# Attention and feed-forward layer on one core: where in each head the next group's key and value projections stand

## What is computed

```
q = (x @ wq) -> 32 heads;  k = (x @ wk), v = (x @ wv) -> 8 heads;   q, k = rope(q), rope(k)
att = softmax(causal(q k^T / sqrt(128)));   x = layernorm(x + (att v) @ wo)
x = layernorm(x + (silu(n @ gate^T) * (n @ up^T)) @ down^T),   n = rmsnorm(x) * ln_w
```

## Time and profile before

| | |
|---|---|
| runs | 1144.85, 1146.91, 1149.17 us, median 1146.91 |
| profiled execution | 1145.77 us, of it 1144.0 us span |
| granted clock of TensorE over the span | 0.994 of full speed |
| busy: PE, DVE, ACT, POOL | 1100.9, 891.5, 643.1, 847.3 us |
| first head ends, seven turns of the loop end | at about 51 and 821 us |

### The profile page before, as it was taken

How to read it: one execution, slowest core, us unless ns; L and a number is a source line. 1 busy time by engine, 2 the same in 40 slices (tenths; PEclk the granted TensorE clock), 3 DMA queues, 4 the chain that set the end, 5 groups by cost and what they waited for, 6 DMA issues and landing times.

```text
span 1144.0 us, 19105 instructions
## 1 busy us (share of the span) xinstructions
PE 1100.9 (96%) x5274; PEld 928.4 (81%) x5274; DVE 891.5 (78%) x1528; ACT 643.1 (56%) x1158; POOL 847.3 (74%) x583
## 2 busy tenths in 40 slices
PE   7899999999999999999999999999998798999997
PEld 6788878887888788878887888788877677888886
DVE  5788787778787878788778777887787888877767
ACT  4666656666666555665666666666655535333333
POOL 1688968996898789878978997899787646544431
PEclk9999999999999999999999999999999998999999
DMA  6855555555555556466646564655554501211101
GB/s 193 229 139 151 138 138 138 153 128 143 143 147 128 138 144 161 115 155 156 155 116 155 152 150 125 162 153 140 129 128 112 153 19 56 74 56 55 37 18 74
DMA packets 155022, 144.60 MB, mean 126 GB/s; under 512 B 15472, under 2 KB 135280, under 8 KB 154992
## 3 DMA queue, kind: packets, MB, share of 16 engines
q1 hardware_dynamic: 142832, 124.31, 42.3%
q10 hardware_dynamic: 12160, 19.93, 6.3%
HBM read 37.23 MB, written 2.10 MB: 34 GB/s over the span
## 4 chain that ended last, share of the span: by engine, by line
PE 71%; POOL 11%; issue 7%; DVE 4%; DMA 3%; ACT 2%; SPq 1%; ACTq 0%; POOLq 0%; DVEq 0%
PE ACC L1516 16%; PE ACC L1517 16%; PE ACC L1518 16%; PE S L1532 4%; PE S L1534 4%; PE S L1533 4%; PE S L1516 4%; PE S L1517 4%; PE S L1518 4%; POOL PT_lo L587 3%; POOL qk_raw L561 2%; POOL rope_s L562 2%; POOL Q_lo L571 1%; POOL wq_lo L540 1%; DMA PT_lo<-turned 1%
## 5 line engine op out<-in xcount | busy, mean ns | idle before, releaser
L1111 DVE CUSTOM_DVE_ANT_0 S<-S,mask 128x128 f32<-128x128 f32 (+7 forms) x256 | 194.0, 758 | 152.4 <-PE S L1534 152.3
L767 ACT ACTIVATE probs<-S,neg_max 128x128 f32<-128x128 f32 (+7 forms) x256 | 189.0, 738 | 201.1 <-DVE neg_max L1111 199.0
L587 POOL TENSOR_TENSOR PT_lo<-PT_lo,PT_hi 128x896 fp32r<-128x896 f32 (+1 forms) x90 | 204.2, 2268 | 19.4 <-ACT PT_hi L774 19.4
L1124 DVE STREAM_TRANSPOSE turned<-probs 128x128 f32<-128x128 f32 (+7 forms) x256 | 197.6, 772 | 1.9 <-ACT probs L767 1.9
L1185 DVE SCALAR_TENSOR_TENSOR y<-ACC,row_rcp,y 128x512 f32<-128x512 f32 x256 | 177.2, 730 | 18.7 <-PE ACC L1518 18.7
L561 POOL TENSOR_TENSOR qk_raw<-qk_raw,cos_sin 128x512 f32<-128x512 f32 x76 | 117.5, 1546 | 78.9 <-DMA rope_s<-qk_raw 78.8
L774 ACT ACTIVATE PT_hi<-PT_lo 128x896 fp32r<-128x896 f32 (+3 forms) x155 | 157.1, 1013 | 24.5 <-DMA PT_lo<-turned 24.2
L1532 PE MATMUL S<-K_hi,Q_hi 128*128 (+4 forms) x380 | 131.6, 346 | 6.4 <-ACT probs L767 4.2
L1516 PE MATMUL ACC<-PT_hi,V_hi 128*128 128x512 f32 x372 | 128.7, 346 | 1.7 <-POOL PT_lo L587 1.5
L1517 PE MATMUL ACC<-PT_lo,V_hi 128*128 128x512 f32 x372 | 129.9, 349 | 0.0
L1518 PE MATMUL ACC<-PT_hi,V_lo 128*128 128x512 f32 x372 | 129.6, 348 | 0.0
(11 more groups left out here) (260 smaller groups left out, 2562.4 us busy)
## 6 DMA issues: line engine op xcount, KB each, us to landing
PT_lo<-turned SPq DMA_DIRECT2D x248, 112.0 KB, 2.5
PT_lo<-turned SPq DMA_DIRECT2D x124, 208.0 KB, 4.1
rope_s<-qk_raw ACTq DMA_DIRECT2D x152, 128.0 KB, 3.7
PT_lo<-turned SPq DMA_DIRECT2D x124, 128.0 KB, 2.6
PT_lo<-turned SPq DMA_DIRECT2D x124, 80.0 KB, 2.3
wq_raw<-in_L_attn_wq_dram SPq DMA_DIRECT2D x32, 256.0 KB, 3.0
wo_raw<-in_L_attn_wo_dram SPq DMA_DIRECT2D x32, 256.0 KB, 3.6
V_stage<-in_L_ffn_down_w_t_dram SPq DMA_DIRECT2D x7, 512.0 KB, 3.6
```

The lines of the kernel that those rows point to most:

```text
L587: nc.gpsimd.tensor_tensor(lo, lo.bitcast(F32), hi.bitcast(F32), ALU.subtract).then_inc(pt_lo_done[half], 1)
L767: nc.scalar.activation(dst, src, ACT.Exp, bias=neg_max[:, at:at + 1], scale=-1.0, accum_out=row_sum[:, j % 2, i:i + 1]).then_inc(exp_done, 1)
L1111: nc.vector.tensor_tensor_reduce(src, src, bias, scale=1.0, scalar=MASKED, op0=ALU.add, op1=ALU.min, accum_out=neg_max[:, at:at + 1]).then ...
L1124: nc.vector.transpose(dst.rearrange("p b (r i) -> p r b i", i=QB), src.rearrange("p (r b i) -> p r b i", b=4, i=QB)).then_inc(turn_done, 1)
```

## The change

The projections of the next group stand at step 2 of heads 1, 2, 3 and 4, one in each. Key half 0 is a head earlier than before, key half 1 too, value half 0 is four steps earlier, value half 1 stays. The `wkv` weights are loaded and split in heads 0, 2 and 4 instead of 1 and 3: `wk` of the second group in the first head, `wv` in head 2, `wk` of the group after the next in head 4 (in the last turn this wraps round to group 0, and nobody uses it). The load stands at step 2 of the head in place of step 1, ScalarE's `wkv_hi` at step 4 in place of 3, POOL's `wkv_lo` at step 5 in place of 4, behind that step's PT_lo.

```diff
-KV_AT = {(2, 2): ("k", 0), (3, 2): ("k", 1), (3, 6): ("v", 0), (4, 2): ("v", 1)}
+KV_AT = {(1, 2): ("k", 0), (2, 2): ("k", 1), (3, 2): ("v", 0), (4, 2): ("v", 1)}
...
             for j, i in FIRST_HEAD:
                 if i == 1:
                     load_wq(2)
+                    sp.dma_start(wkv_raw[:], wk_v[:, :, HD:2 * HD]).then_inc(wkv_in, 16)
...
                 for j, i in LOOP_STEPS:
-                    if i == 1 and j in (1, 3):
+                    if i == 2 and j in (2, 4):
                         sp.wait_ge(wkv_done, g * 2 + (2 + j // 2))
-                        w_v = wk_v if j == 1 else wv_v
-                        sp.dma_start(wkv_raw[:], w_v[:, :, bass.ds(g * HD + HD, HD)]).then_inc(wkv_in, 16)
+                        w_cols = wv_v[:, :, bass.ds(g * HD + HD, HD)] if j == 2 else \
+                            wk_v[:, :, bass.ds((g + 2) % GROUPS * HD, HD)]
+                        sp.dma_start(wkv_raw[:], w_cols).then_inc(wkv_in, 16)
...
-                if i == 4 and not last and j in (1, 3):
-                    split_wkv()
                 for _, half, _, later, _ in ropes_due("sum", j, i, last):
                     rope_sum(half, later)
...
                 if i == 6 and not (last and j >= REP - 2):
                     split_wq()
+                if i == 5 and not last and j in (0, 2, 4):
+                    split_wkv()
...
-                if i == 3 and not last and j in (1, 3):
+                if i == 4 and not last and j in (0, 2, 4):
                     weight_hi("wkv", flat(wkv_hi), flat(wkv_raw), wkv_in)
```

## The result

| | median, us | runs | ratio to before, 95% interval |
|---|---|---|---|
| before | 1147.63 | 4 | |
| changed | 1136.27 (1134.04 to 1139.85) | 4 | 0.991 (0.9886 to 0.9933) |
| changed, measured again (below) | 1137.9 (1136.04 to 1139.56) | 5, beside 21 of before at 1146.67 | 0.9939 (0.9925 to 0.9952) |

The ratios and their intervals are estimated from the single runs; the quotients of the medians are 0.990 and 0.992. Its profiled execution took 1139.85 us (span 1138.0), the slowest of its four, so the two spans are only 6.0 us apart; what is read from them is the groups.

A forecast was written before the change was run, and what follows sets the result against it. TensorE was taken to bound the groups, with time to give only in head 1, waiting mainly for VectorE's additions. Head changes of 14.4 us less 2.1 for POOL gave 12.3 off 1145.77: 1133.5, set at 1134; range 1130.5 to 1140.5.

The forecast's parts named there:

- What each head becomes: TensorE in the groups: heads 1, 2, 3 take 26.80 us each, head 4 27.60; 14.4 us off over seven groups.
- What is late next: Row block 2 and tile 4 scores in head 1 no longer wait; step 6 of head 3 loses cover without a pause.
- POOL, the step that failed in size and place: POOL's queue in head 2: stall of 0 to 1.1 us a group, taken as 0.3; 2.1 us over seven groups.
- ScalarE: ScalarE's queue: wkv_hi a step later and PSUM copies swapped between heads, in steps waiting for VectorE; costs nothing.
- the walk: POOL's queue followed on old head 2's rows: wq_lo ends at 433.65, its query projection started at 433.69, so it just fits.
- the POOL rival: POOL takes the waits over: 1.1 us in head 2, about 0.3 in head 1, 9.8 us in all, 1141; chance 0.12.
- The sum: 14.4 - 2.1 - 0 = 12.3 us off the profiled execution, 1133.5, set at 1134 for the median.
- The rotation of key half 1: Rival: in head 2 it comes late behind the wkv load, 0.9 us on top of the 0.3; 1140 us, chance 0.11.
- hold ScalarE: Rival: a wkv load over 9.35 us delays scores and queries in heads 2 and 4; slower, chance 0.03.
- the wait moves on to the next row block: Rival, nothing moves: the wait for the additions returns at the next row block, head 1 pays 2.72 us; 1146, chance 0.07.

The follow-up runs named there:

- The moved gap: Changed kernel with key half 0 kept in head 1, no projection in head 2, head 3 as before the change: 1149.31 us, ratio 1.0027.
- the late value half: Changed kernel with value half 0 back at step 6 of head 3, everything else as changed: 1152.57 us, ratio 1.0046.
- the help from VectorE: Changed kernel with the PT_lo of step 4 in heads 1 and 2 made by VectorE instead of POOL: 1129.52 us, ratio 0.9856.
- the wkv split taken away: Changed kernel with the wkv split of step 5 in heads 0, 2 and 4 made by VectorE instead of POOL: 1140.74 us, ratio 0.9953.
- VectorE's help in head 2 alone: Changed kernel with the PT_lo of step 4 made by VectorE in head 2 only, POOL keeping it in head 1: 1131.74 us, ratio 0.9877.
- the kernel before with VectorE's help: Kernel before the change with the PT_lo of step 4 on VectorE in heads 2 and 3: 1144.11 us beside 1146.01, ratio 0.9986.

## Why the prediction was right, and which step was not

*What each head becomes.* Heads 1, 3 and 4 were to be 26.80, 26.80 and 27.60 us: in the first profile 26.69 to 26.92 from the second turn on, 26.78 to 26.81, 27.59 to 27.60. The moved gap and the late value half show that the reason is the one given, the cover in step 2. What it covers is two waits, as the prediction had it for head 1, and either can be the long one.

*What is late next.* Nothing in head 1 or in step 6 of head 3, as said. The margin for row block 2 was put at 1.1 us and is 1.8 (384.98 against 383.2).

*POOL, the step that failed in size and place.* I took 0.3 us a group and gave 0 and 1.1 as bounds. Head 2 measures 193.39 us over seven turns in the first profile, 192.74 in the second: 27.6 on average, 0.8 above 26.80, and 5.1 to 5.8 us in all in place of 2.1. Three readings failed.

The start of the chain: I had 0.49 us from old head 3, as a reason for doubt only; it is 0.7 us on average and goes in full to TensorE. Its source I had put at nothing, under "ScalarE": one of the copies that "trade places between heads" does not wait for VectorE but for POOL's Q_lo in head 1.

The place: I walked the queue to its last operation, wq_lo, and read the PT_lo in the middle as "POOL is free at 429.88" without looking who took it: the product at 429.93. TensorE waits there first, ahead of the split.

The end: the walk left wq_lo 0.04 us, and I called that fitting. It is no margin: wq_lo ends at 431.04 in the changed kernel and the query projection starts at 431.10. Both operations are equally late, 3.75 us apart on POOL and their users on TensorE. The wait for PT_lo hides the one for wq_lo: were PT_lo in time and wq_lo not, TensorE would come to the query projection 0.55 us earlier and wait there instead (an estimate from these rows). No run frees PT_lo alone; the help from VectorE makes both earlier, and the wkv split taken away frees wq_lo alone. The one wait of 0.5 us for wq_lo itself is in the seventh turn, 28.21 us, where K_lo waits 0.59 us for ScalarE's K_hi.

The sign that I gave for the POOL rival, a head 2 of 27.5 us or more, came in eight of fourteen turns, with the wait at PT_lo instead of wq_lo. The rival's 1.4 us a group was too much (its 0.2 us of margin is that of old head 2, without the split), the forecast too little.

*The first turn.* Its head 1 took 27.96 and 27.82 us, its head 4 28.00 and 27.98, about 1.5 us together that no step had. In that head 1 some 0.6 us go to the same PT_lo (TensorE waits 0.51 us for it at 73.33): POOL's first rope product comes 0.92 us into the head, behind a wait of 0.98 us for the transfer from the first head. With VectorE's help in head 2 alone this chain begins ahead of the head, and head 1 is at 26.69. Why the transfer is late, and where head 4 loses its 0.4 us, stays open.

*The sum.* Groups 758.1 us were forecast, 763.3 and 762.5 measured: 7.1 to 7.9 us gained, not 12.3. The medians fell by 11.4 and 8.8. What lies outside the groups shows no mark of the change: the first head ends at 47.64 to 49.90 us in the profiles of all the kernels made later, of the kernel before with VectorE's help as well (48.49), against 50.85 in the one of before, which has 1.7 us of half clock in it (last section); what follows the groups took 322.7 us in that profile, 325.6 and 324.1 in the changed kernel's two, 328.5 in the kernel before with help. So about 4 of the first comparison's 11.4 us are no gain of the groups, and that its median of 1136.27 lies so near to 1134 is in part luck of which executions were drawn. 1137.9, from more runs, is the better number: still in the range, but above the forecast's own 1131 to 1137.

*The rivals.* The rotation of key half 1 was not late: its product goes at 420.03, right behind PT_lo, without a wait. The load did not hold ScalarE: at its new place the loads of the loop land in 2.6 to 3.0 us, against 3.8 to 6.2 before. That the wait moves on to the next row block did not happen. The rule of the Trainium skill that the prediction names (DMA: Bandwidth & Descriptors, "Issuing engines are not separate DMA queues": transfers started by different engines run on the same 16 DMA engines) holds here in kind, with 0.65 us of waiting where the load is early, and costs nothing.

## What to carry to other kernels

A wait of the bounding engine that shows in one repetition and not in the next can be a place without cover: put the movable work there, and check by leaving another place empty. Look for a second wait right behind the first, which would take over if only the first were cured. When a queue gets more work, look up each operation's reader in the trace and compare its start with the operation's end; the one that starts just as its input ends has no margin, however much the queue's last operation has. Then take work away ahead of that operation, not behind it: a PT_lo taken out ahead of it in head 2 gave 6 us here, a split behind it none.

## What the runs showed of the hardware

*The same VectorE operation takes 0.66 to 1.80 us, by what POOL does.* The split of 512 columns, line 1211 of the kernel with the wkv split on VectorE (duration ns, shortest, median, longest of 15):

```profile
L1211 DVE TENSOR_TENSOR wkv_lo<-wkv_raw,wkv_hi x15: 656/678/1799, 40.5 to 806.9; 128x512 fp32r<-128x512 f32 x15
```

Five of the six long ones (1.24 to 1.80 us) stand in head 2 beside POOL's Q_lo and PT_lo, the sixth in the first head. The five all end 0.54 to 0.55 us behind the end of Q_lo, however long before it they began. POOL's PT_lo of step 5, 896 columns, takes 2.12 us otherwise and 2.55 to 2.57 beside it. In the two other head 2s the split began just ahead of Q_lo and took 0.66 us, and Q_lo took 1.8 us in place of 1.3. So either side can pay. The Trainium skill (GPSIMD Engine Reference, "Specifications") says that GpSimd shares its SBUF interfaces with VectorE, with contention for VectorE instructions with two SBUF inputs; the trace agrees, with these numbers. So work moved from POOL to VectorE can cost more where POOL goes on working.

*TensorE's clock.* In each profiled execution it falls to half its speed (1.2 GHz in place of 2.4) a few times for short stretches, and where differs. The table by stretch of the kernel before, then of the changed one, at the end of the first head and in the last heads:

```profile
38.00:51.00 13.00, 10.09 (x45) 8.63 (x44) 8.49 (x14) 8.93 (x17) 10.77 (x9) 0.87 0.90 258
876.26:921.26 45.00, 36.47 (x173) 28.13 (x172) 37.76 (x62) 22.79 (x37) 32.62 (x16) 1.00 0.43 120
```
```profile
38.00:51.00 13.00, 10.11 (x50) 8.34 (x50) 8.93 (x17) 9.19 (x18) 11.94 (x10) 1.00 0.89 251
867.38:912.38 45.00, 36.11 (x162) 27.73 (x163) 35.84 (x59) 22.84 (x37) 33.02 (x17) 0.96 0.43 120
```

Before, 13% of the full clock was missing over 13 us at the first head's end, 1.7 us; changed, 4% of 45 us in the last heads, 1.8 us. In both stretches TensorE had been idle for a part of the time. In the groups of these two profiles the granted clock is 1.00 throughout. The changed kernel's two profiles have a mean granted clock of 0.994 and 0.996 over the span, worth 2 to 3 of the 3.8 us between these two executions of one kernel. So such stretches account for a good part of the 4 to 6 us between executions, and no trace here ties one to the change.
